# A recurrence on TensorE: one matmul of the last unit issued ahead of the wait for the state's second half

## What is computed

```python
x = x + attention(rms_norm(x) * (1 + scale(cond)) + shift(cond), 16 heads)
h = cond
for t in range(512):
    r, z, n from gi = x[:, t] @ W_ih + b_ih and gh = h @ W_hh + b_hh:
        r = sigmoid(i_r + h_r);  z = sigmoid(i_z + h_z)
        n = tanh(i_n + r * h_n)
    h = (1 - z) * n + z * h
    out[:, t] = x[:, t] + h
```

## Time and profile before

| | |
|---|---|
| median of 3 runs | 2136.39 us (2132.72 to 2142.32) |
| the profiled execution's own time | 2137.8 us |
| its span, first to last instruction | 2135.5 us |
| busy: PE, PEld | 2106.1 us (99%), 1684.7 us (79%) |
| busy: DVE, ACT, POOL | 1305.2 us (61%), 1130.8 us (53%), 188.2 us (9%) |
| mean granted clock of TensorE | 0.999 of full speed |

### The profile page before, as it was taken

How to read it: one execution, slowest core, us unless ns; L and a number is a source line. 1 busy time by engine, 2 the same in 40 slices (tenths; PEclk the granted TensorE clock), 3 DMA queues, 4 the chain that set the end, 5 groups by cost and what they waited for, 6 DMA issues and landing times.

```text
span 2135.5 us, 130663 instructions
## 1 busy us (share of the span) xinstructions
PE 2106.1 (99%) x58001; PEld 1684.7 (79%) x58001; DVE 1305.2 (61%) x5004; ACT 1130.8 (53%) x5052; POOL 188.2 (9%) x227
## 2 busy tenths in 40 slices
PE   8999999999999999999999999999999999999998
PEld 5665666666888888888888888888888888888776
DVE  4776767666466565666666566656666666656555
ACT  4775766655344454444445444544444454544544
POOL 4433433331000000000000000000000000000000
PEclk9999999999999999999999999999999999999999
DMA  6000000003201000001000001000000100000000
GB/s 225 2 21 2 1 21 2 2 1 135 97 26 27 28 19 25 21 23 27 22 25 21 25 20 29 20 27 19 24 22 25 26 22 25 21 25 21 21 9 9
DMA packets 80574, 62.04 MB, mean 29 GB/s; under 512 B 43596, under 2 KB 75880, under 8 KB 80008
## 3 DMA queue, kind: packets, MB, share of 16 engines
q1 hardware_dynamic: 78960, 50.36, 7.9%
q0 software_dynamic: 528, 3.15, 0.4%
q10 hardware_dynamic: 520, 0.18, 0.0%
HBM read 29.80 MB, written 16.78 MB: 22 GB/s over the span
## 4 chain that ended last, share of the span: by engine, by line
PE 95%; DVE 2%; issue 1%; ACT 1%; POOL 1%; DMA 0%; SPq 0%; DVEq 0%; POOLq 0%
PE ps L658 64%; PE ps L399 7%; PE ps L555 7%; PE ps L491 7%; PE ps L576 3%; PE ps L592 3%; PE ps L461 2%; PE ps L475 1%; PE ps L466 1%; DVE nT L1032 1%; DVE xb L1043 1%; DVE ps L1037 1%; ACT xb L828 1%; DMA x1T<-in_L_cond_W_emb 0%; POOL qk_rs L372 0%
## 5 line engine op out<-in xcount | busy, mean ns | idle before, releaser
L658 PE MATMUL ps<-wqkv,xb 128*4 128x128 f32 x49152 | 1474.4, 273 | 13.2 <-DVE xb L1043 11.8
L658 PEld LDWEIGHTS ps<-wqkv,xb 128*4 128x4 f32 x49152 | 1222.8, 87 | 242.7 <-DVE xb L1043 209.3
L1032 DVE STREAM_TRANSPOSE rzT<-ps 128x128 f32<-128x128 f32 x512 | 162.9, 318 | 362.6 <-PE ps L658 362.6
L833 ACT ACTIVATE r_pair<-rzT 128x8 f32<-128x8 f32 x512 | 107.7, 210 | 481.8 <-DVE rzT L1032 481.8
L1043 DVE TENSOR_TENSOR_SCAN xb<-z_trip,xb 128x24 f32<-128x24 f32 x1024 | 213.0, 208 | 187.8 <-ACT xb L828 130.6
L828 ACT ACTIVATE xb<-ps 128x16 f32<-128x16 f32 x1024 | 190.0, 186 | 132.0 <-DVE ps L1037 121.3
L794 ACT ACTIVATE probs<-ps,negmax 128x512 f32<-128x512 f32 x256 | 173.3, 689 | 102.6 <-DVE negmax L964 102.5
L491 PE MATMUL ps<-wih,x1T 128*32 128x192 f32 x3392 | 222.0, 326 | 0.0
L555 PE MATMUL ps<-wqkv,xnT 128*128 128x384 f32 x512 | 204.4, 487 | 1.0 <-ACT xnT L740 1.0
L840 ACT ACTIVATE z_trip<-znT 128x8 f32<-128x8 f32 x512 | 109.5, 214 | 179.4 <-DVE znT L1032 178.9
L812 ACT ACTIVATE ps<-seeds 128x256 f32<-128x256 f32 x512 | 194.4, 380 | 0.0
(11 more groups left out here) (88 smaller groups left out, 1377.7 us busy)
## 6 DMA issues: line engine op xcount, KB each, us to landing
gi_spill<-gi_image SPq DMA_DIRECT2D x64, 192.0 KB, 2.3
seeds<-gi_spill SPq DMA_DIRECT2D x226, 32.0 KB
seeds<-gi_spill SPq DMA_DIRECT2D x282, 16.0 KB
seeds<-blank SPq DMA_DIRECT2D x10, 384.0 KB, 3.4
out<-xb SPq DMA_DIRECT2D x240, 16.0 KB
xb<-in_x SPq DMA_DIRECT2D x3, 1024.0 KB, 6.8
wih<-in_L_cond_W_ih SPq DMA_DIRECT2D x1, 3072.0 KB, 16.2
seeds<-blank SPq DMA_DIRECT2D x1, 3072.0 KB, 20.5
```

The costliest lines, as they stand in the source:

```text
L658: last = nc.tensor.matmul(ps[QD * j:QD * j + B, bank, 0:P], hist_flat[:, first:first + 3 * B - 2:3], weights, start=False, stop=False, ski ...
L1032: return nc.vector.transpose(into[:].rearrange("p (r k b s) -> p k r s b", r=4, k=blocks, b=B, s=2), ps[:, bank, first:first + QD * blocks])
```

## The change

The eight first-half matmuls of ZN_B were all behind the wait for `h_b` and behind the second halves of the other two units. Now the first of them (chunk 0, strip 0) is issued ahead of that wait, behind the first halves of RZ_A and RB_NA; the other seven stay where they were. `hidden_side` gets a parameter for it. The number of matmuls, their operands, the waits and the signals are the same, except that the sum of the unit in strip 0 gets one of its terms earlier.

```diff
-            def hidden_side(bank, unit, step, half):
-                for k in (2 * half, 2 * half + 1):
+            def hidden_side(bank, unit, step, half, parts=range(8)):
+                for part in parts:
+                    k, j = 2 * half + part // 4, part % 4
                     first = step % HIST * ENTRY + 3 * (1 + B * k) + 1
-                    for j in range(4):
-                        weights = gate_pair(k, unit)[:, :, :, j, :]
...
                 hidden_side(rza_bank, RZ_A, step, 0)
                 hidden_side(rbna_bank, RB_NA, step, 0)
+                hidden_side(znb_bank, ZN_B, step, 0, range(1))
                 pe.wait_ge(s["h_b"], step + 1)
                 hidden_side(rza_bank, RZ_A, step, 1).then_inc(s["rza_sum"], 1)
                 hidden_side(rbna_bank, RB_NA, step, 1).then_inc(s["rbna_sum"], 1)
-                hidden_side(znb_bank, ZN_B, step, 0)
+                hidden_side(znb_bank, ZN_B, step, 0, range(1, 8))
                 hidden_side(znb_bank, ZN_B, step, 1).then_inc(s["znb_sum"], 1)
```

More of the change, by code:

```diff
@@ L651, in gate_pair @@
                 return whh[:, k, :].rearrange("p (g c j x) -> p g c j x", c=KT, j=4, x=QD)[:, gates, chunks, :, :]
-            def hidden_side(bank, unit, step, half):
-                for k in (2 * half, 2 * half + 1):
+            def hidden_side(bank, unit, step, half, parts=range(8)):
+                for part in parts:
+                    k, j = 2 * half + part // 4, part % 4
                     first = step % HIST * ENTRY + 3 * (1 + B * k) + 1
-                    for j in range(4):
-                        weights = gate_pair(k, unit)[:, :, :, j, :]
-                        last = nc.tensor.matmul(ps[QD * j:QD * j + B, bank, 0:P],
-                                                hist_flat[:, first:first + 3 * B - 2:3], weights,
-                                                start=False, stop=False, skip_group_check=True, tile_position=(0, QD * j))
+                    weights = gate_pair(k, unit)[:, :, :, j, :]
+                    last = nc.tensor.matmul(ps[QD * j:QD * j + B, bank, 0:P],
+                                            hist_flat[:, first:first + 3 * B - 2:3], weights,
+                                            start=False, stop=False, skip_group_check=True, tile_position=(0, QD * j))
                 return last
```

## The result

The changed kernel takes **2211.2 us** (median of 6 runs, 2211.07 to 2211.49) where the kernel before takes 2137.6 (2132.72 to 2142.32): a ratio of 1.0347, with a 95% interval of 1.0336 to 1.0357. The profiled execution took 2211.3, its span is 2209.4.

The account below looks back on a forecast made before the run. A closed loop through rza's sum was taken to bound the 3.07 step; 512 x 0.165 = 84.5, less 2 for irregular steps, on 2137.8 gave 2220 us profiled (2218 median), range 2133 to 2232.

Parts of the forecast that it names:

- The bound: Recurrence: a closed loop from restart through rza's sum, rzT, candidate, first state, znT and second state lasts the whole 3.07 step.
- A matmul costs its strip 0.218 and the other strips nothing: At the restart: the extra pair holds strip 0 until 1505.160; strips 1 to 3 can still start at 1504.995.
- The signal waits for strip 0: RZ_A's second half: the signal sent by strip 3's last matmul waits for all earlier matmuls, costing 0.165 rather than zero.
- 0.165 a step: Strip 0 starts rza's second half 0.165 late, making the step 3.23; over 512 steps this is 84.5 us.
- 34 loads before the wait: Sign in a step after: TensorE's weight loads would number 34 before the h_b wait, where 32 came before the stop.
- Relief buys nothing: Behind the wait: strip 0's 0.218 less in znb gains nothing; h_a to h_b may fall from 0.93 to 0.89.
- Two us off for irregular steps: Steps with the state's second half late anyway hide the extra matmul; an estimated 2 us is taken off.
- the signal that doesn't wait: Rival at rza's and rbna's sums: signals follow strip 3, nothing on the loop moves, 2136 us; chance 0.10.
- the pooled stream: Rival at the array: a lone matmul costs 0.055, fits the 0.053 gap, rza starts on time, 2136 us; chance 0.09.
- the faster case: Rival at znT: znb's sum comes sooner, znT follows the first state at 0.09, not 0.13; 2116 us, chance 0.07.
- the queue that holds all strips: Rival at the restart: queue holds the second half until strip 0 takes new weights, 0.06 late; 2167 us, chance 0.07.

## Why the prediction was right, point by point

The stated range, 2133 to 2232, took in the unchanged time as well, so that the result lies in it says little. What bears the forecast out is the step, part by part.

- **The bound** (a closed loop through rza's sum, with rbna's and ZN_B's close by): right. All the growth is ahead of rzT; behind RZ_A the same matmul cost 0.18 a step through rbna.
- **A matmul costs its strip 0.218 and the other strips nothing**: right. Strips 1 to 3 restarted at 1504.88, strip 0 at 1505.06; four cost as one; half the columns cost 0.058, for 0.109 - 0.053 = 0.056 worked out.
- **The signal waits for strip 0**: right, and the weakest step of the prediction. It rested on 0.03 in one step, where the other choice was a price of nothing; that so small a difference pointed the right way was in part luck. The two kernels with another strip or another order gave the 0.03 and 0.05 that counting in program order asks for. Of the rule that the prediction takes from the Trainium skill (TensorE: Matmul & The Clock Gate, Part 3, "What overlaps and what doesn't") these kernels bear out the half on ends: the signal counts in program order. They don't bear out the half on starts: the signal's own matmul starts at 1505.22, the last of strip 0, earlier in program order, at 1505.39.
- **0.165 a step**: right, 3.231 - 3.066 = 0.165. The expectation of how a step would look was right as well for the interval to rzT (0.15 by rows, 0.16 forecast) and rzT to nT (0.37 by rows). Restart to rzT is 0.95 (1504.87 to 1505.82), where 0.93 was forecast. The loads' idle at h_a was forecast at 0.42 and is 0.45, and the forecast "34 loads before the wait" isn't to be seen: the second state now follows the first at 0.90 (1503.71 to 1504.61), while the extra pair still holds strip 0, so loads never pause.
- **Relief buys nothing**: right. znT does come as early as it can, and the interval from h_a to h_b fell from 0.93 to 0.90, not by znT's start (still 0.12 behind the first state) but by its length, 0.29 instead of 0.32. That wasn't foreseen, nor did it matter.
- **Two us off for irregular steps**: this term was mis-sized. It is 8.1. The prediction took these steps for late halves of the state, and put the hidden cost down to those. Its own example, the step at 1541, is another thing: the loads of the step before it stop for 0.25 with no semaphore to wait for, in front of just that one of 256 instructions, the strips run apart from there, and ZN_B's sum and the second half come late by it.

```profile
1540.76 0.20 PEld L658 LDWEIGHTS ps<-wqkv,xb 128*4 128x4 f32 x10 [0.25 <-issue]
```

  Of the 11.0 that the 53 long steps of before take over the median, 6.2 lie in steps that have such a stall of over 0.12 in them or in the step before; in the changed kernel it is 0.5 of 2.8. Most of what is left in the changed kernel is there before as well: five steps, the same ones, each 0.35 over the median. A step of 3.07 with 52 calls runs so near the rate at which instructions come that the irregular steps cost 11.3 in sum; a step of 3.23 leaves room, and they cost 3.2. The spread between runs goes the same way, 9.6 us before and 0.4 in the changed kernel. With the 2.3 by which the first step happened to start sooner this is the difference between 2220 as forecast and 2211.3 as profiled.

The rivals fall by the same rows: the signal that doesn't wait by rzT's 0.60 behind it, the pooled stream by the four strips, the faster case by the extra matmul without relief, the queue that holds all strips by the restart at 1504.88.

## What to carry to other kernels

Price a matmul that uses one column strip by its strip's time, not by a quarter of a set of four: one alone costs as much as four side by side, and the signal of a set waits for the strip that is behind. Before work is put into a gap, measure the gap at the array (rounds of matmuls), not at the weight loads, which here showed 0.16 where the array had 0.05. And count TensorE's instructions in a long unrolled loop as a resource of their own: here four more calls of a few columns, sixteen instructions, put into idle time of a step, cost 87 us.

## What the runs showed of the hardware that was not expected

- TensorE's calls come at no more than one (two loads, two matmuls in fp32) per about 0.058: three kernels with 56 calls a step had mean steps of 3.27 to 3.30, one of them with the order of before untouched. Its stalls stand at one place in every 256 instructions, behind the landing of a 16 KB packet of the instruction queue.
- A signal on a late strip's own matmul comes 0.050 sooner than on one that has six records behind it in program order: 0.008 a record, an estimate from the steps of 3.231 and 3.181.
- A transposition of VectorE from PSUM (`znT`, 128 x 128) takes 0.29 where its sum was there earlier and 0.32 where it starts directly behind it (mean 292 ns in the changed kernel, 316 before; 316 again in the kernel with the extra matmul, whose sum isn't early). The cause is not shown.
- Matmuls of 16 and of 32 columns both leave in rounds of 0.028 for four strips, those of 128 columns in rounds of 0.109.
